# Swin block on one core: TensorE's side jobs regrouped by tile shape, with PSUM banks, element-wise steps and stores placed anew

## Chip, cores and metric

One core of a Trainium2 chip runs the kernel. The metric is the device time of one launch in microseconds, the median of three runs. The kernel before takes 2514.27 us (2513.03 to 2517.35).

## What is computed

The input x is (32, 56, 56, 64) in f32. The reference is one Swin block with shifted 7x7 windows and eight heads of width 8:

```python
y = _ln(x, norm1_w, norm1_b)
y = jnp.roll(y, (-3, -3), axis=(1, 2))
win = y.reshape(B, nWh, 7, nWw, 7, C).transpose(0, 1, 3, 2, 4, 5).reshape(B * nW, N, C)
qkv = (win @ qkv_w.T).reshape(B * nW, N, 3, h, d).transpose(2, 0, 3, 1, 4)
attn = jnp.einsum('bhnd,bhmd->bhnm', q, k) * scale + bias[None]   # + shift mask
attn = jax.nn.softmax(attn, axis=-1)
out = jnp.einsum('bhnm,bhmd->bhnd', attn, v) ... @ proj_w.T + proj_b
x = shortcut + roll(out, (3, 3))
z = _ln(x, norm2_w, norm2_b)
return x + (gelu(z @ fc1_w.T + fc1_b) @ fc2_w.T + fc2_b)
```

## The kernel before, in words

The 2048 windows are cut into NSB = 128 super-blocks of 16 windows. A super-block is worked in U = 8 rounds (k = 0 to 7) of two windows with all heads. Every engine has a program of its own, written by hand as `body(i, m)` for super-block i; the engines meet through semaphores only. VectorE (DVE), ScalarE (ACT), GpSimd (POOL) and SyncE (SP) run four bodies in a hardware loop. TensorE's program is written out in full for all super-blocks.

**The spine.** In round k TensorE does `scores` (tile S, 16 matmuls, in rounds 3 and 7 two more for the mask), `scores_T` of two rounds earlier (tile ST), at most one or two side jobs ("fillers"), `shift` (two matmuls that add the row maximum to ST) and `times_v` of four rounds earlier (tile O). Between them, `neg_max` (VectorE, line 541) takes the row maxima of S, `shift_rows` (GpSimd, 295) makes a diagonal matrix of them, and `exp` (ScalarE, 385) takes the exponential of ST. S has one PSUM bank: `scores` of round k+1 waits for `neg_max` of round k. ST has two.

**The fillers** do the rest of the block for super-blocks at other stages; the letters in `body` name them: a = i+1, f = i+2, n = i+3, c = i-1, d = i-2, e = i-3, g = i-4. `turn_y`, `turn_o`, `turn_z` and `turn_back` are transposes; `project_qk` and `project_v` make q, k and v of the next super-block; `project_out` is the projection behind attention; `fc1` runs in two halves, `fc2` in one. All fillers share the four-bank PSUM tile M.

**Tile shapes.** The part of the array that a matmul uses follows from rows and columns of its weights. The spine's matmuls and `fc2` use all rows and a half of the columns (weights 128x49, 121x49, 113x49, 128x64). The four turns use all rows and all columns (113x128, 128x113). `project_qk`, `project_out` and `fc1` use half of the rows and all columns (64x128, 64x113). `project_v` uses half of both (64x49).

**q and k go through DRAM.** `high_parts` (ScalarE) and `low_parts` (VectorE, 532) split q and k in two f16 parts; `write_parts` (SP) stores them and `read_parts` reads them back, spread over heads, ten transfers a super-block. `scores` of round 0 waits for the first five of them (semaphore `s_q`). SP also issues the loads of x and the stores of the result.

**Other steps.** VectorE: `ln1_*` and `ln2_*` (sums, centering, variance), `evac_yT`, `evac_zT`, `normalise` (twice), `add_attention`, `result`. ScalarE: squares, `place_v`, `evac_oT`, `evac_m`, and `gelu` twice, each change between exp and gelu with a table load. GpSimd: reciprocal roots, row scaling, `keep_residual`.

TensorE's body before, where fillers stand in the rounds:

```python
if k == 0 and on_chip(g): turn_back(g)        # ahead of scores
if k == 0: project_qk(a, d)
if k == 1: project_v(a)
if k == 2: fc1_low(e, a, d)
if k == 3: fc1_high(e, a, g)
if k == 4: turn_y(f, e)      # and fc2(e) behind times_v
if k == 5: turn_o(c, e, a)
if k == 6: project_out(c, f)
if k == 7: turn_z(d, e, a)
```

Of the kernel before, what the change touches and what calls it, by code (L numbers as in the profile page):

```python
# [14 lines left out]
N = WIN * WIN  # L15
SHIFT = 3
HEADS = 8
D = 8
# [3 lines left out]
W0 = 64  # L22
# [18 lines left out]
def swin_block(nc, x, norm1_w, norm1_b, wqk_T, wv_T, proj_wT, proj_b, cpb_w1T, cpb_b1, cpb_w2T, h_times,  # L41
# [4 lines left out]
    with ctx:  # L46
# [162 lines left out]
        def _(sp):  # L209
# [66 lines left out]
        def _(pool):  # L276
# [54 lines left out]
            def body(i, m):  # L331
                f, n, d = i + 2, i + 3, i - 2
                for k in range(U):
                    if k == 0 and on_chip(i):
                        keep_residual(i, m)
                    if on_chip(i):
                        shift_rows(i, k)
                    if k == 1 and on_chip(f):
                        ln1_rows(f)
                    if k == 4 and on_chip(d):  # L340
                        ln2_rstd(d)
                        ln2_rows(d)
                    if k == 7 and on_chip(n):
# [5 lines left out]
        def _(act):  # L349
# [13 lines left out]
            def high_parts(u):  # L363
                act.wait_ge(s_qk, u + 1)
                if later(u):
                    for b in range(2):
                        act.wait_ge(s_parts[b], 32 * u)
                nc.scalar.activation(hl[:, 0].rearrange("m b a t -> m a b t"),  # L368
                                     M[:, 0:2, 0:HT].rearrange("m a (b t) -> m a b t", b=2), ACT.Copy).then_inc(s_hi, 1)

            def place_v(u, r):
                act.wait_ge(s_vp, u + 1)
                dst = vx[r % RING][:].rearrange("n s h f -> n (s h) f")
                for e in range(2):
                    rows = slice(W0 * e, W0 * e + N)
                    nc.scalar.activation(dst[rows, :, D * e:D * e + D].rearrange("n (a s) d -> n a s d", a=2),  # L376
                                         M[rows, 2:4, 0:256].rearrange("n a (s d) -> n a s d", d=D),
# [22 lines left out]
            def gelu(u, c):  # L400
                act.wait_ge(s_f, 2 * u + 1 + c)
                if c == 0 and later(u):
# [4 lines left out]
            def evac_m(u):  # L407
# [3 lines left out]
                nc.scalar.activation(mT[:, :, 0:N], M[:, 2, 0:HT].rearrange("c (w n) -> c w n", n=N),  # L411
                                     ACT.Identity, bias=fc2b[:, 0:1]).then_inc(s_mT, 1)

            def body(i, m):
                a, n, c, d, e = i + 1, i + 3, i - 1, i - 2, i - 3
                for k in range(U):
                    if k == 0 and on_chip(a):
                        high_parts(a)
                    if k == 1 and on_chip(a):
                        place_v(a, m + 1)  # L420
                    u, j = at_unit(i, k, 2)
                    if on_chip(u):
                        exp(u, j)
                    if k == 0 and on_chip(d):
                        square2(d)
                    if k == 2 and on_chip(e):
                        gelu(e, 0)
                        gelu(e, 1)
                    if k == 3 and on_chip(n):
                        square1(n)  # L430
                    if k == 4 and on_chip(c):
                        evac_oT(c)
                    if k == 5 and on_chip(e):
                        evac_m(e)
# [4 lines left out]
        def _(dve):  # L439
# [90 lines left out]
            def low_parts(u):  # L530
                dve.wait_ge(s_hi, u + 1)
                V.tensor_tensor(hl[:, 1].rearrange("m b a t -> m a b t"),
                                M[:, 0:2, 0:HT].rearrange("m a (b t) -> m a b t", b=2),
# [55 lines left out]
            def result(u, r):  # L589
# [3 lines left out]
                V.tensor_tensor(res[r % 2][:], M[0:R, 3, :], xres[r % RING][:].rearrange("r p c -> r (p c)"),  # L593
                                ALU.add).then_inc(s_res, 1)

            def body(i, m):
                a, f, n, c, d, e, g = i + 1, i + 2, i + 3, i - 1, i - 2, i - 3, i - 4
                for k in range(U):
                    if k == 0:
                        if on_chip(d):  # L600
                            ln2_sum(d, m + 2)
                        if on_chip(e):
                            evac_zT(e)
                        if on_chip(c):
                            normalise(c, 0)
                    if k == 4 and on_chip(c):
                        normalise(c, 1)
                    if on_chip(i):
                        neg_max(i, k)
                    if k == 0:  # L610
                        if on_chip(g):
                            result(g, m)
                        if on_chip(d):
                            ln2_center(d, m + 2)
                    if k == 1:
                        if on_chip(a):
                            low_parts(a)
                        if on_chip(d):
                            ln2_var(d)
                    if k == 2 and on_chip(n):  # L620
                        ln1_sum(n, m + 3)
                    if k == 3 and on_chip(n):
# [317 lines left out]
```

## Time and profile before

| | |
|---|---|
| median of three runs | 2514.27 us |
| the profiled execution | 2507.17 us, its span 2505.4 us |
| granted TensorE clock, mean of the span | 0.989 of full speed |
| TensorE busy (PE) | 2260.3 us, 90%, 66954 matmul records (an f32 product that takes two passes counts as two) |
| its weight loads (PEld) | 1741.6 us, 70% |
| GpSimd (POOL) | 1792.0 us, 72% |
| VectorE (DVE) | 1769.7 us, 71% |
| ScalarE (ACT) | 1541.6 us, 62% |
| DMA queue 1 | 138118 packets, 210.58 MB, 41.1% of 16 engines |

Busy time is a union of intervals, and matmuls are pipelined: one matmul's interval covers the starts of those behind it. What a group of matmuls costs TensorE is therefore read from the start of its first matmul to the start of what follows. "issue" names idle time in front of which the profile shows nothing that was waited for.

### The profile page before, as it was taken

The numbers are of one execution on the slowest core, as the hardware profiler recorded it, in microseconds if no ns is written. First come the engines' busy times: TensorE is split into PE (matmuls) and PEld (weight loads), VectorE is DVE, ScalarE is ACT, GpSimd is POOL, SyncE is SP. The second block draws the span as 40 slices with busy tenths as digits, with TensorE's granted clock in tenths as the row PEclk, the third lists the DMA queues.
The fourth block names the chain that finished last, engine by engine and source line by source line (L and its number), as shares of the span: only waits on it lengthen the run. The fifth ranks groups of instructions, "written<-read, shape, count | busy, mean of one in ns | idle before, by whom it ended". The sixth has DMA issues, their size and how long they took to land.

```text
span 2505.4 us, 156242 instructions
## 1 busy us (share of the span) xinstructions
PE 2260.3 (90%) x66954; PEld 1741.6 (70%) x66954; DVE 1769.7 (71%) x3277; ACT 1541.6 (62%) x2433; POOL 1792.0 (72%) x1680
## 2 busy tenths in 40 slices
PE   0528999999999999999999999999999999999998
PEld 0527677777777777777777777776777777777775
DVE  0046777777777777777777777777777877777774
ACT  0005666667666667666766666666667667666665
POOL 0417777777777777777777777777777777777774
PEclk9999999999999999999999999999999999999999
DMA  2014444444444444344444444444444444444441
GB/s 79 0 31 95 87 94 90 94 93 97 93 99 90 98 90 93 86 95 94 101 89 100 87 100 87 94 90 94 89 88 95 95 95 98 91 91 92 90 93 41
DMA packets 138664, 219.38 MB, mean 88 GB/s; under 512 B 30182, under 2 KB 96476, under 8 KB 137948
## 3 DMA queue, kind: packets, MB, share of 16 engines
q1 hardware_dynamic: 138118, 210.58, 41.1%
q8 instruction: 528, 8.65, 1.6%
q14 instruction: 18, 0.15, 0.0%
HBM read 133.40 MB, written 77.07 MB: 84 GB/s over the span
## 4 chain that ended last, share of the span: by engine, by line
PE 83%; issue 5%; ACT 5%; SPq 2%; DVE 2%; POOL 1%; DMA 0%; ACTq 0%; DVEq 0%; POOLq 0%
PE O L706 13%; PE ST L692 11%; PE S L670 9%; PE M L714 8%; PE ST L686 8%; PE M L779 7%; PE M L801 7%; PE M L765 5%; PE M L748 5%; PE M L732 5%; PE M L809 3%; ACT L404 3%; ACT gl L404 2%; SPq L220 2%; PE S L648 2%
## 5 line engine op out<-in xcount | busy, mean ns | idle before, releaser
L295 POOL TENSOR_TENSOR nmd<-diag,nm 121x392 f16<-121x392 f16 x1024 | 898.0, 885 | 443.6 <-DVE nm L541 423.3
L541 DVE TENSOR_REDUCE nm<-S 121x8 f16<-121x392 f32 x1024 | 576.5, 563 | 385.6 <-PE S L674 185.5
L385 ACT ACTIVATE pT<-ST 113x392 f32<-113x392 f32 x1024 | 506.4, 495 | 408.2 <-PE ST L692 403.7
L706 PEld LDWEIGHTS O<-vx,pT 113*49 113x49 f32 x16384 | 552.0, 127 | 62.7 <-issue 21.9
L706 PE MATMUL O<-vx,pT 113*49 113x18 f32 x16384 | 529.8, 197 | 18.7 <-issue 16.2
L686 PE MATMUL ST<-qp,kp 128*49 128x49 f16 x16384 | 396.7, 186 | 30.2 <-issue 28.1
L670 PE MATMUL S<-kp,qp 128*49 128x49 f16 x16384 | 395.9, 186 | 25.6 <-issue 16.1
L670 PEld LDWEIGHTS S<-kp,qp 128*49 128x49 f16 x16384 | 318.8, 104 | 98.5 <-issue 70.2
L692 PE MATMUL ST<-nmd,shiftw 121*49 121x392 f16 x2048 | 362.6, 350 | 1.4 <-POOL nmd L295 0.9
L686 PEld LDWEIGHTS ST<-qp,kp 128*49 128x49 f16 x16384 | 330.3, 103 | 42.8 <-issue 34.2
L692 PEld LDWEIGHTS ST<-nmd,shiftw 121*49 121x49 f16 x2048 | 107.3, 101 | 285.3 <-issue 144.3
L368 ACT ACTIVATE hl<-M 128x784 f16<-128x784 f32 x128 | 105.5, 824 | 278.7 <-PE M L732 278.7
L315 POOL TENSOR_TENSOR xres<-xin,projb 113x512 f32<-113x512 f32 x128 | 204.9, 1601 | 94.5 <-DVE res L593 90.8
L302 POOL TENSOR_TENSOR rstd<-veps,mhalf 113x8 f32<-113x8 f32 x128 | 209.6, 1637 | 83.2 <-DVE veps L521 83.2
L779 PE MATMUL M<-zT,w 64*128 64x392 f32 x1024 | 246.8, 555 | 3.6 <-issue 1.9
L404 ACT ACTIVATE gl<-M,b 128x784 f32<-128x784 f32 x256 | 220.8, 911 | 4.9 <-PE M L779 3.4
L322 POOL TENSOR_TENSOR rstd<-veps,mhalf 113x8 f32<-113x8 f32 x128 | 210.9, 1648 | 12.2 <-DVE veps L580 12.2
L801 PE MATMUL M<-gl,w 128*64 128x392 f32 x1024 | 194.0, 500 | 3.4 <-ACT gl L404 3.4
L376 ACT ACTIVATE vx<-M 49x512 f32<-49x512 f32 x256 | 155.2, 606 | 33.6 <-PE M L748 24.0
L404 ACT ACT_TABLE_LOAD x126 | 161.7, 1283 | 2.3
L385 ACT ACT_TABLE_LOAD x126 | 161.7, 1283 | 2.2
L547 DVE RECIPROCAL rec<-O 113x32 f32<-113x32 f32 x256 | 90.2, 352 | 85.0 <-PE O L706 85.0
(93 smaller groups left out, 3406.0 us busy)
## 6 DMA issues: line engine op xcount, KB each, us to landing
parts<-hl SPq DMA_DIRECT2D x512, 98.0 KB, 2.7
qp<-parts SPq DMA_DIRECT2D x512, 98.0 KB
xin<-in_x SPq DMA_DIRECT2D x256, 98.0 KB
kp<-parts SPq DMA_DIRECT2D x256, 98.0 KB
kp<-parts SPq DMA_DIRECT2D x512, 49.0 KB
out<-res SPq DMA_DIRECT2D x256, 98.0 KB
onehot<-in_c_onehot SPq DMA_DIRECT2D x2, 2082.5 KB
w<-in_fc_wT SPq DMA_DIRECT2D x3, 64.0 KB
```

Of the source, the lines that this page charges most:

```text
L295: nc.gpsimd.tensor_tensor(nmd[j % LAG][:], diag[:], nm[j % LAG][:].unsqueeze(2).broadcast_to([RM, 2 * 4, N]), ALU.mult).then_inc(s_nmd, 1)
L302: nc.gpsimd.tensor_tensor(rstd1[:], veps1[:], mhalf[:], ALU.pow).then_inc(s_rs1, 1)
L322: nc.gpsimd.tensor_tensor(rstd2[:], veps2[:], mhalf[:], ALU.pow).then_inc(s_rs2, 1)
L385: nc.scalar.activation(pT[j % LAG][:].rearrange("k w h q -> k (w h q)"), ST[0:R, j % 2, 0:HK], ACT.Exp).then_inc(s_e, 1)
L404: nc.scalar.activation(gl[:, c], M[:, 2 * c:2 * c + 2, 0:HT], ACT.Gelu, bias=b1[:, c:c + 1]).then_inc(s_g, 1)
L541: V.tensor_reduce(nm[j % LAG][:], S[0:RM, 0:HK].rearrange("q (h n) -> q h n", n=N), AX_X, ALU.max, negate=True).then_inc(s_nm, 1)
L670: mm = MM(S[W0 * e:W0 * e + N, N * (4 * w + hp):N * (4 * w + hp + 1)], q[:, 2 * hp + e, t], key[:, 2 * hp + e, t], start=(w == 0 and hp == ...
L686: MM(ST[W0 * e:W0 * e + N, j % 2, N * (4 * w + hp):N * (4 * w + hp + 1)], key[:, 2 * hp + e, t], q[:, 2 * hp + e, t], start=(w == 0 and hp ...
L692: mm = MM(ST[W0 * e:W0 * e + N, j % 2, 0:HK], shiftw[:, variant(r, j), e, :], nmd[j % LAG][:].rearrange("r h n -> r (h n)"), start=False, ...
L706: mm = MM(O[W0 * w:W0 * w + N, (4 * p + hp) * VC:(4 * p + hp + 1) * VC], pT[j % LAG][:, w, hp, :], vx[r % RING][:, window + w, hp, :], sta ...
L779: mm = MM(M[:, 2 * c + h, 0:HT], w1[rows, 128 * c:128 * c + 128], zT[rows, :], start=True, stop=True)
L801: mm = MM(M[C * h:C * h + C, 2, 0:HT], w2[:, c, :], gl[:, c, h, :], start=(c == 0), stop=(c == 1), tile_position=(0, C * h), skip_group_ch ...
```

## The change

The computation and its instructions are the same, but for their order, the PSUM bank that each filler uses, and the semaphores that guard the banks.

- TensorE: `project_out` moves from round 6 into round 0 behind `project_qk` (both with weights of 64 rows); all four turns stand together in round 5; `turn_z` and `fc1` go one stage later (fc1 in rounds 6 and 7, high half first), and `fc2` moves to round 4, for g. Rounds 1 and 3 have no filler, `project_v` is in round 2.
- Banks of M: q and k in banks 2 and 3 (were 0 and 1), v in 0 and 1 (were 2 and 3), fc2 and `turn_back` in bank 0 (were 2 and 3).
- VectorE: `neg_max` comes first in each round; `low_parts` moves from round 1 to round 2, `add_attention` from round 6 to round 0 of the next body, `evac_zT`, `result` and `ln2_var` into round 5 behind `evac_yT`.
- ScalarE: its fillers stand ahead of `exp` in their round; gelu in round 7 in place of 2.
- GpSimd: `ln2_rstd` in round 0, `ln1_rows` and `ln2_rows` in round 2, `keep_residual` in round 5, `ln1_rstd` in round 6.
- SP: the store of the result is issued behind the transfers of q and k, not ahead of them.

```diff
@@ sync body
             if on_chip(n):
                 load(n, m + 3)
-            if on_chip(g):
-                store(g, m)
             if on_chip(a):
                 write_parts(a, m + 1)
                 read_parts(a, m + 1, 0)
                 read_parts(a, m + 1, 1)
+            if on_chip(g):
+                store(g, m)
@@ scalar body
-                    if k == 0 and on_chip(a):
+                    if k == 1 and on_chip(a):
                         high_parts(a)
-                    if k == 1 and on_chip(a):
+                    if k == 3 and on_chip(a):
                         place_v(a, m + 1)
+                    if k == 4 and on_chip(g):
+                        evac_m(g)
+                    if k == 4 and on_chip(c):
+                        evac_oT(c)
+                    if k == 5 and on_chip(d):
+                        square2(d)
+                    if k == 5 and on_chip(n):
+                        square1(n)
+                    if k == 7 and on_chip(e):
+                        gelu(e, 1)
+                        gelu(e, 0)
                     u, j = at_unit(i, k, 2)
                     if on_chip(u):
                         exp(u, j)
...
@@ vector body, as it stands now
                    if on_chip(i):
                        neg_max(i, k)
                    if k == 0:
                        normalise(c, 0); add_attention(d, m + 2)
                    if k == 1: ln2_sum(d, m + 2)
                    if k == 2: low_parts(a); ln1_sum(n, m + 3)
                    if k == 3: normalise(c, 1)
                    if k == 4: ln1_center(n, m + 3); ln2_center(d, m + 2)
                    if k == 5: evac_yT(f); evac_zT(e); result(g, m); ln2_var(d)
                    if k == 6: ln1_var(n)
@@ tensor: the guards that changed
-            def project_qk(u, d):
+            def project_qk(u, d, g):
                 pe.wait_ge(s_yT, u + 1)
-                if on_chip(d):
-                    pe.wait_ge(s_att, d + 1)
+                if on_chip(g):
+                    pe.wait_ge(s_g, 2 * g + 1)
...
-                    mm = MM(M[:, h, 0:HT], wqk[rows, :], yT[rows, :], start=True, stop=True)
+                    mm = MM(M[:, 2 + h, 0:HT], wqk[rows, :], yT[rows, :], start=True, stop=True)
...
+            def project_out(u, i, g):
                 pe.wait_ge(s_oT, u + 1)
+                if on_chip(g):
+                    pe.wait_ge(s_g, 2 * g + 2)
...
+            def fc2(u, a, d):
+                pe.wait_ge(s_g, 2 * u + 2)
                 if on_chip(a):
+                    pe.wait_ge(s_vx, 2 * a + 2)
@@ tensor body
                     if k == 0 and on_chip(a):
-                        project_qk(a, d)
-                    if k == 1 and on_chip(a):
+                        project_qk(a, d, g)
+                    if k == 0 and on_chip(d):
+                        project_out(d, i, g)
+                    if k == 2 and on_chip(a):
+                        room_for_v(a, d)
                         project_v(a)
...
+                    if k == 4 and on_chip(g):
+                        fc2(g, a, d)
+                    if k == 5:
+                        if on_chip(f):
+                            turn_y(f, a)
+                        if on_chip(c):
+                            turn_o(c, a)
+                        if on_chip(e):
+                            turn_z(e, a)
+                        if on_chip(g):
+                            turn_back(g)
+                    if k == 6 and on_chip(e):
+                        fc1_high(e, c)
+                    if k == 7 and on_chip(e):
+                        fc1_low(e, f, g)
                     if on_chip(u2):
                         shift(u2, r2, j2)
                     if on_chip(u4):
                         times_v(u4, r4, j4)
-                    if k == 4 and on_chip(e):
-                        fc2(e)
```

How TensorE's order changes, first around rounds 0 to 2. A row is a group of matmuls; S, ST and O are the spine's tiles. Before, from round 0 (behind its `turn_back`):

```order
L670 MATMUL S<-kp,qp 49x49 x16
L686 MATMUL ST<-qp,kp 49x49 x16
L732 MATMUL M<-yT,wqk 128x392 x2
L692 MATMUL ST<-nmd,shiftw 49x392 x2
L706 MATMUL O<-vx,pT 49x18 x8
L670 MATMUL S<-kp,qp 49x49 x16
L686 MATMUL ST<-qp,kp 49x49 x16
L748 MATMUL M<-wv,yT 49x32 x32
L692 MATMUL ST<-nmd,shiftw 49x392 x2
L706 MATMUL O<-vx,pT 49x18 x8
L670 MATMUL S<-kp,qp 49x49 x16
L686 MATMUL ST<-qp,kp 49x49 x16
```

And the same place now:

```order
L737 MATMUL M<-yT,wqk 128x392 x2
L770 MATMUL M<-wproj,oT 113x64 x8
L694 MATMUL ST<-nmd,shiftw 49x392 x2
L708 MATMUL O<-vx,pT 49x18 x8
L672 MATMUL S<-kp,qp 49x49 x16
L688 MATMUL ST<-qp,kp 49x49 x16
L694 MATMUL ST<-nmd,shiftw 49x392 x2
L708 MATMUL O<-vx,pT 49x18 x8
L672 MATMUL S<-kp,qp 49x49 x16
L688 MATMUL ST<-qp,kp 49x49 x16
L751 MATMUL M<-wv,yT 49x32 x32
```

The projection stands directly behind q and k, a whole round of the spine without a filler comes in between, and v is one round later. The same engine at the turns of round 5, where the spine stood between any two of them before:

```order
L688 MATMUL ST<-qp,kp 49x49 x16
L716 MATMUL M<-ident,y 128x113 x4
L716 MATMUL M<-ident,on 128x113 x4
L716 MATMUL M<-ident,z 128x113 x4
L814 MATMUL M<-ident,mT 113x128 x4
L694 MATMUL ST<-nmd,shiftw 49x392 x2
L708 MATMUL O<-vx,pT 49x18 x8
```

The four turns now follow one another with nothing between. On VectorE, this is what stands between the maxima of rounds 5, 6 and 7 now:

```order
L528 TENSOR_SCALAR yT<-M,n1w,n1b 128x392
L587 TENSOR_SCALAR zT<-M,n2w,n2b 128x392
L594 TENSOR_TENSOR res<-M,xres 113x512
L577 TENSOR_REDUCE ss<-sq 113x8
L581 TENSOR_SCALAR veps<-ss 113x8
L542 TENSOR_REDUCE nm<-S 121x8
L518 TENSOR_REDUCE ss<-sq 113x8
L522 TENSOR_SCALAR veps<-ss 113x8
L542 TENSOR_REDUCE nm<-S 121x8
```

Behind the turns, five steps are queued ahead of round 6's maximum, where before it was one or two.

## Rows read from the trace of the kernel before

**Rows 1.** Busy time by stretch, 400 to 1000 us: length, busy (matmuls counted), clock, DMA share, GB/s; and the page's row of instruction transfers
```profile
400.00:1000.00 600.00, 578.71 (x17602) 443.33 (x17602) 458.67 (x844) 407.67 (x642) 464.33 (x439) 0.99 0.47 94
...
q8 instruction: 528, 8.65, 1.6%
```

**Rows 2.** Waits of PE: waiter, released by, us in total, times, longest
```profile
PE ST L686 <- issue: 28.1, 37, 2.3
PE O L706 <- issue: 16.2, 22, 2.4
PE S L670 <- issue: 16.1, 30, 1.5
PE M L714 <- ACT gl L404: 12.9, 56, 0.5
```

**Rows 3.** Timeline of PE, round 7: start us, us, line, operation, tiles, count
```profile
1217.38 0.38 PE L686 MATMUL ST<-qp,kp 128*49 128x49 f16 x16
1217.69 0.61 PE L714 MATMUL M<-ident,z 113*128 113x113 f32 x4
1218.22 0.35 PE L692 MATMUL ST<-nmd,shiftw 121*49 121x392 f16 x2
```

**Rows 4.** Timeline of PE, a stretch that ends within a turn (its first two matmuls)
```profile
1231.57 0.37 PE L670 MATMUL S<-kp,qp 128*49 128x49 f16 x16
...
1232.08 0.41 PE L714 MATMUL M<-ident,on 113*128 113x113 f32 x2
```

**Rows 5.** Timeline of PE, rounds 1 and 2 of the next super-block, v to fc1
```profile
1221.91 0.94 PE L748 MATMUL M<-wv,yT 64*49 64x32 f32 x64
1222.77 0.35 PE L692 MATMUL ST<-nmd,shiftw 121*49 121x392 f16 x2
1222.96 0.51 PE L706 MATMUL O<-vx,pT 113*49 113x18 f32 x16
1223.31 0.37 PE L670 MATMUL S<-kp,qp 128*49 128x49 f16 x16
1223.52 0.27 PE L686 MATMUL ST<-qp,kp 128*49 128x49 f16 x8
1224.76 0.29 PE L686 MATMUL ST<-qp,kp 128*49 128x49 f16 x8 [0.97 <-issue]
1224.98 0.93 PE L779 MATMUL M<-zT,w 64*128 64x392 f32 x4
1225.84 0.35 PE L692 MATMUL ST<-nmd,shiftw 121*49 121x392 f16 x2
```

**Rows 6.** Timeline of PE near the start, where a round had no filler
```profile
196.18 0.21 PE L670 MATMUL S<-kp,qp 128*49 128x49 f16 x2 [0.30 <-DVE nm L541]
```

**Rows 7.** Timeline of DVE: that round's maximum, and later the one of Rows 4
```profile
195.57 0.55 DVE L541 TENSOR_REDUCE nm<-S 121x8 f16<-121x392 f32 x1
...
1231.98 0.57 DVE L541 TENSOR_REDUCE nm<-S 121x8 f16<-121x392 f32 x1 [1.50 <-PE S L670]
```

**Rows 8.** Timeline of DVE, from result on in the super-block of Rows 5
```profile
1220.47 0.68 DVE L593 TENSOR_TENSOR res<-M,xres 113x512 f32<-113x512 f32 x1
1221.07 0.68 DVE L571 SCALAR_TENSOR_TENSOR z<-sum,xres 113x512 f32<-113x512 f32 x1
...
1223.26 0.68 DVE L576 TENSOR_REDUCE ss<-sq 113x8 f32<-113x512 f32 x1
1223.97 0.55 DVE L580 TENSOR_SCALAR veps<-ss 113x8 f32<-113x8 f32 x1
1224.43 0.55 DVE L541 TENSOR_REDUCE nm<-S 121x8 f16<-121x392 f32 x1
```

**Rows 9.** Timeline of PE, the projection behind attention
```profile
1215.61 1.01 PE L765 MATMUL M<-wproj,oT 64*113 64x64 f32 x16
```

**Rows 10.** The first trip of q and k through DRAM: low parts on DVE, then PE's wait
```profile
174.77 0.97 DVE L532 TENSOR_TENSOR hl<-M,hl 128x784 f16<-128x784 f32 x1 [1.84 <-ACT hl L368]
...
185.04 0.56 PE L670 MATMUL S<-kp,qp 128*49 128x49 f16 x16 [8.17 <-DMA kp<-parts]
```

More of the change, by code:

```diff
@@ L400, in gelu @@
             def gelu(u, c):
-                act.wait_ge(s_f, 2 * u + 1 + c)
-                if c == 0 and later(u):
+                act.wait_ge(s_f, 2 * u + 2 - c)
+                if c == 1 and later(u):
                     act.wait_ge(s_m, u)
@@ L423, in body @@
                         exp(u, j)
[L424 to L434, printed above, removed]
             rounds(act, body)
@@ L610, in body @@
                     if k == 0:
+                        if on_chip(c):
+                            normalise(c, 0)
+                        if on_chip(d):
+                            add_attention(d, m + 2)
+                    if k == 1 and on_chip(d):
+                        ln2_sum(d, m + 2)
+                    if k == 2:
+                        if on_chip(a):
+                            low_parts(a)
+                        if on_chip(n):
+                            ln1_sum(n, m + 3)
+                    if k == 3 and on_chip(c):
+                        normalise(c, 1)
+                    if k == 4:
+                        if on_chip(n):
+                            ln1_center(n, m + 3)
+                        if on_chip(d):
+                            ln2_center(d, m + 2)
+                    if k == 5:
+                        if on_chip(f):
+                            evac_yT(f)
+                        if on_chip(e):
+                            evac_zT(e)
                         if on_chip(g):
@@ L716, in turn_tokens, with turn_y, room_for_v @@
                 mm.then_inc(sem_out, 1)
[L718 removed]
+            def turn_y(u, a):
                 pe.wait_ge(s_y1, u + 1)
[L720 to L723 removed]
+                if on_chip(a):
+                    pe.wait_ge(s_vx, 2 * a + 2)
                 turn_tokens(1, y1, s_yTp)
[L726 removed]
+            def project_qk(u, d, g):
                 pe.wait_ge(s_yT, u + 1)
+                if on_chip(g):
+                    pe.wait_ge(s_g, 2 * g + 1)
+                else:
+                    if on_chip(d):
+                        pe.wait_ge(s_oT, d + 1)
+                    if later(u):
+                        pe.wait_ge(s_lo, u)
+                for h in range(2):
+                    rows = slice(C * h, C * h + C)
+                    mm = MM(M[:, 2 + h, 0:HT], wqk[rows, :], yT[rows, :], start=True, stop=True)
+                mm.then_inc(s_qk, 1)
+            def room_for_v(u, d):
                 if on_chip(d):
                     pe.wait_ge(s_att, d + 1)
[L730 to L737 removed]
                 elif later(u):
                     pe.wait_ge(s_vx, 2 * u)
[L740 to L741 removed]
             def project_v(u):
@@ L819, in body @@
                     r4 = m if k >= 4 else m + 3
-                    if k == 0 and on_chip(g):
-                        turn_back(g)
                     if on_chip(i):
                         scores(i, m, k)
-                    if k == 1 and on_chip(a):
-                        room_for_v(a, e, g)
                     if on_chip(u2):
```

129 lines of the change are left out of this document (42 added, 87 removed).

## The prediction

> **What bounds the kernel now.** I read the busy shares first. In the 600 us of [rows 1] TensorE is busy for 578.71, VectorE for 458.67, GpSimd for 464.33, ScalarE for 407.67. Then the waits [rows 2]: where TensorE stands still, it mostly waits for nothing that the profile shows ("issue"), and next for gelu. So its own stream sets the end. Its length comes from start to start. [rows 1] count 17602 matmul records in 600 us; a super-block has 523 (66954 of the table above, by 128), so it takes 17.8 us.
>
> **Unit.** Everything below is in us per super-block, and times 127 at the end (128, less what start and tail have out of step).
>
> **Term 1, changes of tile shape: -0.93.** In [rows 3] the turn begins 0.31 behind the start of ST's 16 matmuls. Where the same shape goes on, such a group passes on after 0.21 (S to ST in [rows 5], 1223.31 to 1223.52). Going in costs 0.10. The first step in the turn is long too: two matmuls of a turn are busy 0.41 [rows 4], four 0.61 [rows 3], so the later ones are 0.10 apart, and the first two 0.41 less the 0.27 of one, which is 0.14. Going out: the turn lasts 0.53 from start to start, its four starts spread over 0.14 + 0.10 + 0.10 = 0.34, and what follows comes 0.19 behind the last in place of 0.10. One separate filler thus pays 0.10 + 0.04 + 0.09 = 0.23 for its shape. Before there are nine such visits (turn_back, q and k, v, fc1 twice, y, o, projection, z), now five (q and k with the projection, v, the four turns, fc1 twice); fc2 has the spine's shape in both. Four visits fewer, 4 x 0.23 = 0.93. Bounds: 0.40 if only the way in is saved, 1.1 if each visit is read 0.04 too low. I take 0.93, since the rows show both sides.
>
> **Term 2, the wait for gelu: -0.15.** turn_y waited for gelu to free its bank, 12.9 us in 56 times [rows 2], 0.10; waits too short for the list make it somewhat more (bounds 0 and 0.2). Now y waits for v's evacuation, rounds earlier. Gelu sits in round 7, and q and k of the next round 0 wait for its first half: a tie, which I count as nothing.
>
> **Term 3, S has one bank: +0.35.** A round without filler is 0.21 (S) + 0.21 (ST, as S) + 0.19 (shift) + 0.35 (O) = 0.96, all from [rows 5]. The loop S, maximum, S needs 0.41 from S's start to the maximum's (1231.57 [rows 4] to 1231.98 [rows 7]) and 0.61 from there to the next S (195.57 [rows 7] to 196.18 [rows 6]), together 1.02. Rounds 1 and 3 lose 0.06 to 0.10 each. Round 6 is worse. Behind the last turn VectorE has result 0.60, the variance 0.71 and 0.46, all start to start [rows 8], 1.8 in all; S of round 6 starts about 0.6 after turn_back ends, so its maximum starts some 1.4 later and the next S 0.61 after that, 2.0 to 2.1, where a round with fc1 lasts 0.21 + 0.31 + 0.86 + 0.19 + 0.35 = 1.92 (fc1 0.86 from [rows 5]). That is 0.1 to 0.2 more. Together 0.35, bounds 0.1 and 0.6.
>
> **Term 4, instructions come in pieces: +0.42.** The profile counts 528 instruction transfers for 2 x 66954 matmuls and weight loads [rows 1]: 254 instructions each, nearly all TensorE's. [rows 5] show what such a piece costs. In the 2.2 us up to 1223.7 about 128 matmuls with as many loads went out, then nothing for 0.97: a piece takes some 3.2 us to arrive (estimate from these rows), and a stretch that uses 256 instructions faster than that stops for the difference. The densest stretch before runs from q and k's end to fc1: 36 + 64 + 128 + 36 + 64 = 328 instructions in 2.9 us (a spine group of 16 is 32, v is 128). Now it runs from the projection's end to fc2: 36 + 100 + 64 + 128 + 36 + 104 + 64 = 532 instructions in 5.0 us, since rounds 1 and 3 are bare. A piece of 256 lies wholly within such a stretch (328 - 256) / 256 = 0.28 times a super-block before, and (532 - 256) / 256 = 1.08 times now. The three largest issue rows of [rows 2] are 60.4 us in 89 times, 0.68 a time, 0.47 a super-block, with the small ones near 0.58. I reckon the new sum as 1.08 x 0.68 + 0.25 for pieces that fall elsewhere = 1.0. Bounds: nothing, and 0.8 x 0.97 = 0.78. I take 0.42, nearer to the middle since some dense pieces pass without a stop.
> The Trainium skill says the reverse ("Runtime: NRT & Kernel Launch", Instruction fetch mechanics): crossing a 16 KiB boundary, 256 instructions, is mostly hidden. The trace does not agree, with 60.4 us in three rows. By that rule the term would be zero, the sum -0.74 and the time that of rival A.
>
> **Small terms: -0.01.** The stops of term 4 fall into rounds 1 to 3 and cover part of term 3's waits there, -0.06; the clock, 0.99 in [rows 1], may be granted a little less with more stops, +0.05.
>
> **Costed at nothing.** *q and k through DRAM*: round 0 is 0.21 + 0.31 + 0.86 (q and k, as fc1 in [rows 5]) + about 0.8 (the projection, busy 1.01 with its last matmul's tail [rows 9]) + 0.54 = 2.7, round 1 1.0, and low_parts starts behind round 2's maximum (0.41 + 0.48), 4.6 after round 0's S. The next round 0 comes 16.2 after it if nothing stops (17.8, less 0.6 of issue, 0.2 of clock, 0.93 and 0.15, plus 0.35, in round numbers). The first trip took 10.3 from low_parts to S [rows 10]. So 1.3 is left, and any stop adds to it; with that gone it is rival C. *VectorE in round 0*: it holds the maximum, one normalise and add_attention, and has 2.7. *GpSimd*: eight shift_rows and five steps stay; each result is due two rounds later, at least 1.4 after it is made. *ScalarE*: gelu with its table loads lies between two exps; exp of round 7 ends about when round 1's ST asks for it, where TensorE would wait for the maximum anyway. *Stores*: issued later on SP, behind q and k, with no reader. *Start and tail*: the same chain of steps, 1 us either way.
>
> **Sum.** -0.93 - 0.15 + 0.35 + 0.42 - 0.01 = -0.32, times 127 is -41 us. Against the profiled execution, 2507.2, that is 2466; the median of the runs stands 7.1 above it, so 2473.
>
> **Rivals.**
> *A. Instructions are no hindrance.* Then -0.74, -94 us: 2420. For it: some dense pieces pass freely. Against: the stops of [rows 2]. 0.22.
> *B, slower: the dense stretch starves TensorE.* Each of the 1.08 dense pieces stops for 0.97 as in [rows 5], the total goes to 1.35 with the rest, +0.78; with more stops the clock may stand at its lower level more often, for which I put 0.4 (the 0.99 of [rows 1] is a loss of 0.2). With term 3 at 0.4 it comes to -0.93 - 0.15 + 0.4 + 0.78 + 0.4 = +0.50, +64 us: 2578. It decides from +0.74 on for terms 4 and clock together; just past that point lies 2515 to 2540. For it: two bare rounds around the densest filler. 0.17.
> *C. q and k's trip.* The 10.3 of [rows 10] was on DMA engines with little else to do. If it is 12 under load, each super-block waits about 0.5 at S of round 0, in part in place of term 3: 2520. 0.08.
> *D. The turns cool the clock.* The four turns now take 1.8 us without an ordinary matmul. If the clock fell behind them, rounds 6 and 7 (3.9 us) would run at the lower level, where S's group is busy 0.56 [rows 10] in place of 0.37 [rows 5], half as long again: +2.0, +250 us, 2725. The 0.99 of [rows 1], with four separate turns, speaks against it. 0.03.
> The Trainium skill has the rule behind D ("TensorE: Matmul & The Clock Gate", Part 4: PE-mode transpose): transposes do not count as busy for the clock the way matmuls do. No run so far shows turns side by side.
> *E. The change of shape is not what costs* in term 1, and neighbours save nothing: -0.15 + 0.35 + 0.42, +79 us, 2593. 0.02.
>
> **Numbers.** The forecast has 0.48, its own range 2440 to 2505. With A below and the near part of B and C above, 2405 to 2545 leaves out about 2 in 10. A difference under 0.2%, 5 us, is about what a measurement of this kernel can't tell from none. Faster: 0.48 + 0.22 = 0.70; same 0.07, the edge of B and C; slower 0.23.
>
> **What would show it.** *Term 1*: the four turns take 1.7 to 1.8 us from start to start, and the projection starts right behind q and k (under 0.8 after them). *Term 3*: "DVE nm" as releaser of S in rounds 2, 4 and 7, some tens of us. *Term 4*: issue waits grow from about 75 to about 125 us, mostly in rounds 1 to 4. *Wrong*: issue unchanged (A), issue over 170 us or a clock under 0.97 (B, D), "DMA kp<-parts" in front of S (C), or waits for ScalarE's pT in round 1.

## The result, and the profile after

The changed kernel takes 2558.86 us (median of 4 runs, 2542.95 to 2566.67), beside 2513.65 us for the kernel before in the same comparison. The ratio is 1.019, with an interval of 1.011 to 1.027: it is slower by 1.9%. I had forecast 2473 us with a range of 2405 to 2545, and gave "slower" 0.23. The profiled execution is 2542.95 us, 35.8 above the one before.

The page's first rows and its chain, of the kernel after:

```profile
PE 2187.6 (86%) x66954; PEld 1756.8 (69%) x66954; DVE 1877.4 (74%) x3277; ACT 1515.4 (60%) x2433; POOL 1760.8 (69%) x1680
...
PE 66%; DVE 15%; issue 13%; SPq 2%; POOL 2%; DMA 1%; DVEq 0%; ACT 0%; POOLq 0%; ACTq 0%
```

TensorE is busy 73 us less than before (2260.3) and the span is 36 us longer. So the change of order did shorten TensorE's work, and more than all of it came back as standing still. Of the chain, VectorE has 15% and "issue" 13%.

The waits of PE, kernel after (waiter, released by, us in total, times, longest):

```profile
PE S L672 <- DVE nm L542: 43.1, 126, 1.0
PE ST L688 <- issue: 40.9, 47, 1.7
PE M L751 <- issue: 39.5, 54, 1.2
PE S L672 <- issue: 36.0, 43, 1.6
...
PE O L708 <- issue: 28.9, 30, 1.5
```

Against [rows 2]: the gelu wait of the turn (12.9 us) is gone. A wait for VectorE's maximum, once in nearly every super-block, has come. All issue rows together are 156.2 us, where they were 75.6. The row M L751 is `project_v`.

Timeline of PE, kernel after, one super-block from round 0 to the end of round 6 (start us, us, line, operation, tiles, count):

```profile
1236.37 0.37 PE L672 MATMUL S<-kp,qp 128*49 128x49 f16 x16
...
1236.89 0.93 PE L737 MATMUL M<-yT,wqk 64*128 64x392 f32 x4
1237.65 0.92 PE L770 MATMUL M<-wproj,oT 64*113 64x64 f32 x16
...
1239.03 0.37 PE L672 MATMUL S<-kp,qp 128*49 128x49 f16 x16
...
1240.15 0.39 PE L672 MATMUL S<-kp,qp 128*49 128x49 f16 x16
...
1240.69 0.46 PE L751 MATMUL M<-wv,yT 64*49 64x32 f32 x19
1241.70 0.74 PE L751 MATMUL M<-wv,yT 64*49 64x32 f32 x45 [0.56 <-issue]
...
1244.04 0.36 PE L672 MATMUL S<-kp,qp 128*49 128x49 f16 x13
1245.08 0.23 PE L672 MATMUL S<-kp,qp 128*49 128x49 f16 x3 [0.68 <-issue]
...
1247.74 0.60 PE L716 MATMUL M<-ident,y 113*128 113x113 f32 x4
1248.18 0.55 PE L716 MATMUL M<-ident,on 113*128 113x113 f32 x4
1248.57 0.55 PE L716 MATMUL M<-ident,z 113*128 113x113 f32 x4
1248.96 0.60 PE L814 MATMUL M<-ident,mT 128*113 128x128 f32 x4
1249.49 0.35 PE L694 MATMUL ST<-nmd,shiftw 121*49 121x392 f16 x2
...
1250.03 0.37 PE L672 MATMUL S<-kp,qp 128*49 128x49 f16 x16
...
1252.41 0.40 PE L672 MATMUL S<-kp,qp 128*49 128x49 f16 x16 [0.32 <-DVE nm L542]
```

Read the neighbours first. The projection starts 0.76 after q and k (1236.89 to 1237.65), and the turns step by 0.44, 0.39, 0.39 and 0.53, which is 1.75. Now the bare round 1, from 1239.03 to 1240.15, is 1.12 long. Then two stops: within `project_v`, and within S of round 4. Each stretch between two starts is longer than the idle time in brackets, since the last matmuls' tails count as busy. Last, round 6 runs from 1250.03 to 1252.41, 2.38, and ends on a wait for the maximum.

The means say the same over the run. These are the lengths from S to the next S in us, the mean of 95 super-blocks (20 to 114), worked out from both traces:

```
round      0     1     2     3     4     5     6     7    sum
before   2.01  2.09  2.28  2.14  3.14  1.65  2.12  2.51  17.94
after    2.69  1.16  2.54  1.61  2.81  2.96  2.44  2.06  18.26
```

DVE and POOL of the kernel after, the same place, from VectorE's center steps to round 6's maximum:

```profile
1246.43 1.33 DVE L572 SCALAR_TENSOR_TENSOR z<-sum,xres 113x512 f32<-113x512 f32 x1
...
1249.76 0.68 DVE L594 TENSOR_TENSOR res<-M,xres 113x512 f32<-113x512 f32 x1
1250.36 0.68 DVE L577 TENSOR_REDUCE ss<-sq 113x8 f32<-113x512 f32 x1
1251.07 0.81 DVE L581 TENSOR_SCALAR veps<-ss 113x8 f32<-113x8 f32 x1
1251.80 0.55 DVE L542 TENSOR_REDUCE nm<-S 121x8 f16<-121x392 f32 x1
```

```profile
1245.99 1.22 POOL L295 TENSOR_TENSOR nmd<-diag,nm 121x392 f16<-121x392 f16 x1 [0.95 <-DVE nm L542]
...
1250.59 1.27 POOL L315 TENSOR_TENSOR xres<-xin,projb 113x512 f32<-113x512 f32 x1 [1.43 <-DVE res L594]
```

The maximum starts 1.77 after its S (1250.03). The step `veps` ahead of it takes 0.73 from start to start, where [rows 8] have 0.46, and it ends at 1251.88, together with GpSimd's `keep_residual` (1251.86).

**Where stops fall.** Count TensorE's matmuls, weight loads and semaphore instructions through from the first of the trace, in pieces of 256. Between 400 and 2300 us, 93 steps before and 252 after last over 0.45 us from one start to the next, waits for other engines among them. Of these 73 and 157 stand at one and the same place of a piece, and no other place has more than 3. So the time in which one piece was used can be set against the stop behind it, both from start to start. Pieces used in 2.0 to 2.5 us: 29 before, with a mean stop of 0.89; 88 after, with 1.11. Pieces that took 4 us or more have next to none in either trace (means 0.09 and 0.08). The kernels have 436 and 429 pieces in that time. The transfers can be counted through in the same way: in both traces the instruction at that place never starts less than 2.17 us behind the start of its transfer, in 390 pieces each. This is the picture of term 4, with about a fifth of all pieces dense instead of a fifteenth.

### The profile page after: what moved, and what is told of

Read it like the earlier page. It is cut to its first block, busy times and chain, and to the rows that moved or that the text cites. A ratio compares the mean times of both kernels' runs of the same rounds, so it can differ in the third digit from the quotient of the medians.

```text
span 2541.1 us, 156517 instructions
## 1 busy us (share of the span) xinstructions
PE 2187.6 (86%) x66954; PEld 1756.8 (69%) x66954; DVE 1877.4 (74%) x3277; ACT 1515.4 (60%) x2433; POOL 1760.8 (69%) x1680
## 4 chain that ended last, share of the span: by engine, by line
PE 66%; DVE 15%; issue 13%; SPq 2%; POOL 2%; DMA 1%; DVEq 0%; ACT 0%; POOLq 0%; ACTq 0%
PE O L708 10%; PE S L672 10%; PE ST L688 7%; PE ST L694 7%; PE M L806 6%; PE M L716 5%; PE M L751 5%; PE M L737 4%; PE M L782 4%; PE M L770 4%; DVE ss L577 3%; DVE nm L542 3%; DVE res L594 2%; SPq L220 2%; DVE zT L587 2%
## 5 line engine op out<-in xcount | busy, mean ns | idle before, releaser
L386 ACT ACTIVATE pT<-ST 113x392 f32<-113x392 f32 x1024 | 498.1, 498 | 396.5 <-PE ST L694 393.0
L708 PEld LDWEIGHTS O<-vx,pT 113*49 113x49 f32 x16384 | 561.3, 127 | 97.3 <-issue 57.4
L672 PE MATMUL S<-kp,qp 128*49 128x49 f16 x16384 | 406.6, 187 | 93.6 <-DVE nm L542 43.1
L315 POOL TENSOR_TENSOR xres<-xin,projb 113x512 f32<-113x512 f32 x128 | 162.4, 1269 | 170.2 <-DVE res L594 170.2
L302 POOL TENSOR_TENSOR rstd<-veps,mhalf 113x8 f32<-113x8 f32 x128 | 210.7, 1646 | 97.0 <-DVE veps L522 83.7
L782 PE MATMUL M<-zT,w 64*128 64x392 f32 x1024 | 237.2, 541 | 0.5 <-DVE zT L587 0.3
L412 ACT ACTIVATE mT<-M,fc2b 128x392 f32<-128x392 f32 x128 | 76.4, 597 | 251.6 <-PE M L806 251.6
L806 PE MATMUL M<-gl,w 128*64 128x392 f32 x1024 | 204.3, 513 | 6.9 <-issue 3.9
L393 ACT ACTIVATE oT<-M 128x452 f32<-128x452 f32 x128 | 70.0, 547 | 182.2 <-PE M L716 182.2
L751 PE MATMUL M<-wv,yT 64*49 64x32 f32 x8192 | 136.0, 210 | 39.6 <-issue 39.5
L572 DVE SCALAR_TENSOR_TENSOR z<-sum,xres 113x512 f32<-113x512 f32 x128 | 166.8, 1303 | 0.0
L405 ACT ACT_TABLE_LOAD x126 | 161.7, 1283 | 2.2
```

The source lines that it names most:

```text
L302: nc.gpsimd.tensor_tensor(rstd1[:], veps1[:], mhalf[:], ALU.pow).then_inc(s_rs1, 1)
L386: nc.scalar.activation(pT[j % LAG][:].rearrange("k w h q -> k (w h q)"), ST[0:R, j % 2, 0:HK], ACT.Exp).then_inc(s_e, 1)
L405: nc.scalar.activation(gl[:, c], M[:, 2 * c:2 * c + 2, 0:HT], ACT.Gelu, bias=b1[:, c:c + 1]).then_inc(s_g, 1)
L672: mm = MM(S[W0 * e:W0 * e + N, N * (4 * w + hp):N * (4 * w + hp + 1)], q[:, 2 * hp + e, t], key[:, 2 * hp + e, t], start=(w == 0 and hp == ...
L708: mm = MM(O[W0 * w:W0 * w + N, (4 * p + hp) * VC:(4 * p + hp + 1) * VC], pT[j % LAG][:, w, hp, :], vx[r % RING][:, window + w, hp, :], sta ...
L751: mm = MM(M[W0 * e:W0 * e + N, h, 32 * s:32 * s + 32], yT[rows, N * s:N * s + N], wv[rows, e, :], start=True, stop=True, tile_position=(C ...
```

## Experiments

In each, lines with a minus stood in the kernel named first. All ratios are to the kernel before, on the same chip, with their 95% interval.

**1. The variance of ln2 later.** The changed kernel, with the last two of the five VectorE steps ahead of round 6's maximum (`ln2_var`, its sum and `veps`) moved behind round 7's.

```diff
@@ vector body, k == 5
                             result(g, m)
-                        if on_chip(d):
-                            ln2_var(d)
@@ behind k == 6
+                    if k == 7 and on_chip(d):
+                        ln2_var(d)
```

> The changed kernel with one step of VectorE moved: the variance step ln2_var goes from round 5 (ahead of round 6's maximum) to round 7 (behind its maximum). Theory V (round 6 waits for a maximum that is queued behind result and ln2_var; in the changed kernel's trace the median length of round 6 is 2.47 us where its work needs 1.92): round 6 falls to 1.9 to 2.0, 0.5 us in each of 128 super-blocks, 45 to 65 us faster than the changed kernel, so about 2495 to 2515. Rival I (only the issue stops of TensorE, 156 us in the changed kernel against 76 before, are to blame and would fill any gap that VectorE leaves): less than 15 us faster.

Measured: 1.0057 (1.0027 to 1.0088), 1.3% below the change's 1.0189, some 33 us and less than expected. Round 6 has a mean of 1.95, 0.49 less. Its waits of PE:

```profile
PE ST L688 <- issue: 43.8, 51, 1.7
...
PE M L751 <- issue: 31.7, 56, 2.1
...
PE M L737 <- ACT gl L405: 10.2, 65, 0.4
```

The maximum is gone from the list's head, so VectorE's queue ahead of round 6 is shown to be one of the two causes. Not all of the 0.49 is a gain. Round 0 grew from 2.69 to 2.99, since q and k now reach their bank before gelu has left it. This is the tie that I had counted as nothing.

**2. The projection in the bare round 1.** The changed kernel, with `project_out` (and `add_attention`, which reads it) moved from round 0 to round 1. This splits the dense stretch and gives up one pair of neighbours.

```diff
@@ tensor body
-                    if k == 0 and on_chip(d):
+                    if k == 1 and on_chip(d):
                         project_out(d, i, g)
```

> The changed kernel with project_out moved from round 0 to the bare round 1 (and add_attention of VectorE with it). It costs one more visit of another tile shape, about 0.2 us a super-block (+25 us), and cuts the dense stretch of TensorE's instructions from 532 to 432. Theory I (instruction pieces of 256 that are used up in under 3.5 us stop TensorE for about 1 us each): the pieces that lie wholly in the dense stretch fall from 1.08 to 0.69 a super-block, issue waits fall from 156 to 105 to 120 us, and the time falls by 10 to 35 us net, to about 2525 to 2550. Rival (stops do not follow from the density around v): issue unchanged, time 20 to 30 us longer, 2580 to 2590.

Measured: 1.0306 (1.0231 to 1.0381). Its waits of PE:

```profile
PE S L671 <- DVE nm L542: 56.4, 151, 1.0
...
PE O L707 <- DVE on L552: 26.6, 118, 1.1
PE ST L687 <- issue: 24.7, 33, 1.4
```

Issue falls to 84 us in all from 156, near the 75.6 of the kernel before. That is term 4's cause shown by taking it away: same instructions, one bare round less beside v. Part of the fall can be due to the new waits in these rounds, in which instructions come in as well. And yet the time went up, by 1.2%, which is at the edge of the noise. Rounds 0 and 1 together take 4.52 in the mean for 3.85. Of that, 0.30 is the extra visit (the steps of q and k, ST, shift and the projection, from start to start). Most of the rest is a new wait, with 26.6 us of idle time and more from start to start: round 0 takes 2.30 where its steps add up to 1.91. `times_v` of round 0 writes over what `normalise` reads, and the projection had stood between.

**3. One turn moved in the kernel before.** `turn_y` (and `evac_yT`) from round 4 to round 5, beside `turn_o`.

```diff
@@ tensor body of the kernel before
-                    if k == 4 and on_chip(f):
+                    if k == 5 and on_chip(f):
                         turn_y(f, e)
```

> The kernel BEFORE with one pair of turns side by side: turn_y goes from round 4 to round 5, directly ahead of turn_o (evac_yT of VectorE with it). No round becomes bare, since fc2 stands in round 4. Theory S (a visit of another tile shape costs 0.23 us) plus the wait of turn_y for gelu, 0.15, which goes: 0.38 us a super-block, 40 to 50 us faster than before, so 2465 to 2475. Rival (side by side saves nothing; the gain is eaten by other waits): 0 to 20 us faster.

Measured: 1.0143 (1.0062 to 1.0224). One wait of PE stands out:

```profile
PE O L706 <- DVE on L551: 45.9, 124, 0.6
```

The turn steps by 0.44 beside its neighbour, so the pair saves as forecast, and the gelu wait is gone. But `turn_y` had been what covered `normalise(c, 1)` in round 4, and this wait costs more than its idle time: without the turn the steps of round 4 add up to 2.29 from start to start, and the median is 2.89. That is 0.60 lost, against 0.21 for the pair and 0.16 for gelu.

**4. Two pairs.** The same with `turn_z` behind round 7's `times_v`, right ahead of `turn_back`.

```diff
@@ tensor body
-                    if k == 7 and on_chip(d):
-                        turn_z(d, e, a)
@@ behind times_v and fc2
+                    if k == 7 and on_chip(d):
+                        turn_z(d, e, a)
```

> The previous one with a second pair: turn_z goes from ahead of shift in round 7 to the end of round 7, directly ahead of turn_back. Theory S: a further 0.23 us a super-block, 25 to 30 us, so 2435 to 2448, with issue waits near the 76 us of the kernel before. Rival: no further gain, the same as the previous one within 8 us.

Measured: 1.0112 (1.0075 to 1.0149). The intervals of this and of experiment 3 overlap, so the second pair's worth can't be read from them; the next experiment has it alone.

**5. turn_z beside turn_back alone.** The kernel before with the second edit only, and `evac_zT` behind round 0's maximum.

```diff
@@ vector body, k == 0
-                        if on_chip(e):
-                            evac_zT(e)
@@ behind neg_max, k == 0
+                        if on_chip(e):
+                            evac_zT(e)
```

> The kernel BEFORE with one pair only: turn_z at the end of round 7, directly ahead of turn_back, and VectorE's evac_zT behind round 0's maximum, so that the later turn delays no maximum. turn_y keeps its place in round 4, where it covers the wait of times_v for normalise (26 to 47 us of waits in the two kernels that had taken that cover away). Theory S: 0.23 us a super-block, 25 to 30 us faster than before (ratio 0.988 to 0.990), issue waits unchanged at 70 to 90 us. Rival (a pair saves nothing net): ratio 0.997 to 1.01.

Measured: 0.9974 (0.9935 to 1.0012), which can't be told from no change. Round 7 is 0.26 shorter in the mean (2.25), as a pair should make it, and round 1 is 0.21 longer (2.30): `evac_zT` pushes VectorE's later steps, and round 1's maximum starts 0.87 behind its S in the median, instead of 0.50. Pair and queue cancel.

**6. fc1 as a pair.** The kernel before with both halves of fc1 in round 2 and round 3 bare. The bare round stands apart from v here.

```diff
@@ tensor body of the kernel before
-                    if k == 3 and on_chip(e):
+                    if k == 2 and on_chip(e):
                         fc1_high(e, a, g)
```

> The kernel BEFORE with both halves of fc1 in round 2, so that round 3 is bare, but not beside v: the two halves of fc1 stand between. Theory: -0.23 for the visit, -0.15 for turn_y's wait for gelu, +0.1 for the S loop of the bare round, together -0.28, 30 to 40 us faster than before (ratio 0.984 to 0.988), issue waits stay at 70 to 90 us. Rival (any bare round starves TensorE): issue waits over 110 us, ratio over 1.

Measured: 1.0191 (1.0129 to 1.0253). Its first wait of PE, and the timeline of ACT (an exp of round 2, gelu with its two table loads, the next exp):

```profile
PE M L714 <- ACT gl L404: 118.9, 123, 1.2
```

```profile
1236.06 0.50 ACT L385 ACTIVATE pT<-ST 113x392 f32<-113x392 f32 x1 [2.21 <-PE ST L692]
1236.58 1.28 ACT L404 ACT_TABLE_LOAD   x1
1237.88 1.72 ACT L404 ACTIVATE gl<-M,b 128x784 f32<-128x784 f32 x2
1239.61 1.28 ACT L385 ACT_TABLE_LOAD   x1
1240.90 0.50 ACT L385 ACTIVATE pT<-ST 113x392 f32<-113x392 f32 x1
```

Rounds 2 and 3 together are 4.06 in the mean against 4.42 before. Against that, `turn_y` waits for gelu 0.97 us each time. Issue is 65 us, so a bare round in this place adds no stops. That it is the place which matters, and not the count of bare rounds, isn't shown by this run alone: TensorE also stands still for gelu right behind the bare round, and its next instructions can come in meanwhile.

**7. Both.** Experiments 5 and 6 in one kernel.

> Both of the previous edits together on the kernel BEFORE. Theory: the gains add to 0.5 us a super-block, ratio 0.974 to 0.980 to before, and it beats both kernels. Rival (a wait for VectorE or ScalarE takes the second gain): ratio 0.985 or above.

Measured: 1.0169 (1.0084 to 1.0254), with the gelu wait of experiment 6 (120.0 us).

**8. fc1 as a pair in round 3, round 2 bare beside v.** Meant to feed the dense stretch in the kernel before; gelu moves to round 3 as well.

```diff
@@ tensor body of the kernel before
-                    if k == 2 and on_chip(e):
+                    if k == 3 and on_chip(e):
                         fc1_low(e, a, d)
@@ scalar body: gelu twice, behind square1
-                    if k == 2 and on_chip(e):
+                    if k == 3 and on_chip(e):
```

> As the fc1 pair, but both halves in round 3, so that the bare round 2 stands directly behind v: the dense stretch grows from 328 to 432 instructions with the same matmuls and the same pair. Theory I (density around v): issue waits rise to 110 to 140 us, 35 to 60 us above those of the fc1 pair in round 2; turn_y and round 4 also wait for the later gelu, some 1 to 2 us a super-block, so the time is well above before (ratio 1.03 to 1.10) and only the issue waits are compared. Rival: issue waits the same as in the pair of round 2, within 15 us.

Measured: 1.2061 (1.1994 to 1.2127). The size of it was foreseen by no theory. Its timeline of PE around the wait, and behind it:

```profile
1236.32 0.98 PE L714 MATMUL M<-ident,y 113*128 113x113 f32 x4 [2.74 <-ACT gl L404]
...
1237.56 0.82 PE L706 MATMUL O<-vx,pT 113*49 113x18 f32 x16
```

`turn_y` stands still for 2.74 us, and what follows runs at the lower clock: O's group is busy 0.82 where it is 0.51 elsewhere. Two stretches behind it (length, busy of PE, PEld, DVE, ACT, POOL, clock, DMA share, GB/s):

```profile
1236.30:1241.50 5.20, 5.18 (x59) 3.08 (x61) 0.73 (x2) 2.46 (x3) 1.76 (x2) 0.50 0.47 79
1243.00:1248.00 5.00, 5.00 (x165) 4.45 (x162) 3.79 (x8) 1.93 (x5) 2.76 (x3) 1.00 0.02 3
```

So the gelu chain costs twice, once as a wait (331.7 us in all) and again at 1.2 GHz behind it. Issue is 61 us, but the super-block is now 22 us long, and while TensorE waits for gelu its next instructions come in. This run doesn't settle what it was made for.

**9. Both mends of the change.** Experiments 1 and 2 in one kernel.

> Both single mends of the change together: ln2_var in round 7 and the projection in round 1 (its attention sum with it). Theory 'separate causes' (VectorE's queue ahead of round 6's maximum, and the instruction supply of the stretch with two bare rounds, add up): issue falls to about 85 us as with the projection moved alone, round 6 stays near 1.95 us as with the variance moved alone, and the one new wait of the projection's move stays (times_v of round 0 waits for normalise, about 27 us). Ratio to the kernel before about 1.0057 + 0.0117 = 1.017, less if q and k wait less for gelu. Rival 'one cause' (the stops only shift work against the VectorE queue): issue stays at 120 us or more once round 6 is short again.

Measured: 1.0241 (1.0177 to 1.0304). Issue is 72 us and round 6 1.95, so the two causes are separate. The sum of the single effects, 1.017, lies just below the interval, but has noise of about 0.01 of its own, so the ratios don't show that the two together cost more. The trace has a wait that neither had, while the one for `normalise` is down to 5.8 us:

```profile
PE ST L687 <- ACT pT L386: 57.1, 112, 1.5
```

**10. Experiment 9 with normalise ahead of round 0's maximum.**

```diff
@@ vector body
+                    if k == 0 and on_chip(c):
+                        normalise(c, 0)
                     if on_chip(i):
                         neg_max(i, k)
-                    if k == 0:
-                        if on_chip(c):
-                            normalise(c, 0)
```

> As the one before, with normalise of round 0 ahead of round 0's maximum on VectorE, as the kernel before has it. Theory: round 0 holds q and k (about 1.9 us), so its maximum may come 0.4 us later at no cost, and the wait of times_v for normalise (about 27 us) goes away: 15 to 27 us less than with normalise behind the maximum, ratio 1.005 to 1.01. Rival: the maximum becomes late instead, S of round 1 waits for it, and the time is the same within 0.3%.

Measured: 1.0201 (1.0172 to 1.0229), which can't be told from experiment 9. The wait for normalise is gone (1.3 us) and round 0 is 2.10 instead of 2.33; the wait for exp takes it over (87.7 us). Timeline of ACT, and under it the matmuls that wait:

```profile
1239.49 1.28 ACT L405 ACT_TABLE_LOAD   x1
1240.79 1.72 ACT L405 ACTIVATE gl<-M,b 128x784 f32<-128x784 f32 x2
1242.53 1.28 ACT L386 ACT_TABLE_LOAD   x1
1243.82 0.89 ACT L386 ACTIVATE pT<-ST 113x392 f32<-113x392 f32 x2
```

```profile
1244.37 0.40 PE L686 MATMUL ST<-qp,kp 128*49 128x49 f16 x16 [0.76 <-ACT pT L386]
```

Gelu with its table loads holds ScalarE for 4.3 us (1239.49 to 1243.82). TensorE can be only two rounds ahead of exp, as ST has two banks, and rounds 7 and 0 are now 4.2 together. What the slow rounds 6 and 0 of the changed kernel had hidden is the next bound. The Trainium skill ("ScalarE: Activation LUTs", What ACT_TABLE_LOAD costs) puts a switch at 1283 ns for the load plus a drain of about 1380 ns. The load agrees, 1.28 here; in both timelines what follows a load starts 0.01 to 0.02 us behind it, so no drain shows on this path.

**11. Gelu ahead of exp.** Experiment 6 with gelu twice ahead of round 2's exp on ScalarE.

> The kernel before with both fc1 halves in round 2 and gelu ahead of round 2's exp on ScalarE. Theory 'late start': the wait of turn_y for gelu (119 us with gelu behind exp) is there since gelu starts only behind an exp that itself waits for shift; ahead of it gelu starts at fc1's end, 1 us or more earlier, the wait falls under 40 us and the ratio to 1.000 to 1.006. Rival 'ScalarE's block': gelu twice with two table loads is some 4.5 us, and the exp behind it then comes late for times_v two rounds on: TensorE waits for pT (O) or for ST's bank in rounds 3 to 5, 60 us or more, and the ratio stays above 1.012.

Measured: 1.1208 (1.1179 to 1.1237). The gelu wait is gone and a greater one stands in its place, so the rival "ScalarE's block" holds. It costs more than the wait itself, again with a lower clock (0.934):

```profile
PE ST L686 <- ACT pT L385: 221.1, 125, 2.2
```

**12. The same with turn_z beside turn_back.**

> The same with turn_z beside turn_back as well (which alone gave 0.9974). Theory 'late start': 0.995 to 1.003, the best of the versions with pairs. Rival 'ScalarE's block': above 1.01, with the waits for exp's result named above.

Measured: 1.1208 (1.1190 to 1.1227), with the same wait (237.0 us). No version with pairs is shown to beat the kernel before.

## Why the prediction was wrong

The steps, in us per super-block. "Measured" is read from the profiled executions.

| step | predicted | measured |
|---|---|---|
| term 1, visits | -0.93 | -1.09 (15.50 for 16.59, all steps without stops and waits) |
| term 2, gelu wait of the turn | -0.15 | gone, -0.10 in the list, -0.16 from start to start |
| term 3, round 6 | +0.1 to 0.2 | +0.52 (2.44 for 1.92) |
| term 3, rounds 1 and 3 | +0.06 to 0.10 each | +0.16 (1.12 for 0.96) and +0.09 (1.13 for 1.04, with the mask's two matmuls) |
| term 4, issue | +0.42 | +0.63 as idle time (80.6 us by 127), +0.79 from start to start |
| sum | -0.32 | +0.28 (35.8 us by 127), +0.32 in the mean super-block |

From start to start the measured terms add to -1.09 - 0.16 + 0.52 + 0.25 + 0.79 = +0.31, and the mean super-block grew by 0.32. So terms 3 and 4 failed, and the saving was even larger than forecast. That stops and waits would cover one another (the -0.06) isn't seen.

**Term 1 was right, and it wasn't the step that failed.** The projection comes 0.76 behind q and k ("under 0.8") and the turns take 1.75 ("1.7 to 1.8"). A visit is 0.27 where I had read 0.23, and the four make the 1.1 of the bound. Rival E is out. The fc1 pair of experiment 6 tells the price again: round 2 grew by less than round 3 lost, 0.36 in the mean with a stop or two among it. In the medians rounds 2 and 3 are 2.57 and 1.13 for 1.93 and 2.00, 0.23 less, although the bare round loses some 0.1 to the loop.

**Term 3 failed by its size**, 0.77 where I had 0.35, above my bound of 0.6. Its round 6 rests on 1.8 us of VectorE's steps [rows 8] and on S starting 0.4 behind `result`. In the sample S came 0.27 behind it, and the steps took 0.60 + 0.71 + 0.73 = 2.04. The 0.27 more lies in `veps`, beside a `keep_residual` that this change had moved to the very place. It is held up until `keep_residual` ends (last section), and the row of [rows 8] was a held one too. I costed GpSimd's move at nothing since its results had slack, and didn't ask what it does to VectorE while it runs. Experiment 1 shows that this queue is worth 1.3%. The bare rounds failed by the loop's 0.41 from S to the maximum: it is 0.50 there (1239.03 to 1239.53), and 0.62 from it to the next S. The 0.41 came from round 5. In rounds 0, 1, 3 and 7 of the kernel before, the median was 0.50 to 0.52 already.

**Term 4 was right in mechanism and too small.** The number of dense pieces came: 122 of the 429 were used in under 3 us, 1.17 a super-block for my 1.08. I took 0.68 a stop from [rows 2]. That is a mean of idle time over stops of all kinds, and those of the densest pieces last 1.11 from start to start (88 of them). Rival B had 0.97 for this and +0.78, and from start to start +0.79 came. Experiment 2 takes the stops away and with them 72 us of idle time. Rival B's other leg, the clock, didn't come: 0.988 against 0.989. So the time, 2559 us, lies near the rival's 2578 by a partly different sum, without its 0.4 for the clock and with 0.77 for its 0.4 of term 3. The Trainium skill's "mostly hidden" ("Runtime: NRT & Kernel Launch", Instruction fetch mechanics) doesn't hold here: the stops are 156 us of a 2541 us span, and rival A is out.

**Costed at nothing.** q and k through DRAM: TensorE waits for kp 11.2 us in 3 times, the longest 7.3, where a stall in each super-block was rival C, so C is out. The turns and the clock: D is out, no fall behind 1.75 us of turns. ScalarE: a tie as I said, but hidden only by the losses of term 3. When experiments 1 and 9 mend those, it costs 10.2 us at gelu, then 57.1 at exp. I had let one wait stand as cover for another ("where TensorE would wait for the maximum anyway"), and that cover goes as soon as the first wait is mended.

**Still open.** Why some GpSimd instructions hold `veps` up and its reciprocal roots don't, no run here shows. A kernel that has all of term 1 and none of the uncovered waits was not tried.

## What to carry over

Price each move twice: once for what the job costs in its new place, and once for the latency that it used to cover in the old one, on each engine that had it between a request and its answer. Work out the slack of every other engine against the time hoped for, not the time before. A duration read from a trace holds for the neighbours that it had there: look for the same instruction at its shortest. Where a stream is issued from instructions fetched in pieces, sparse fillers (few long matmuls) do a second job beside dense ones, and a saving that removes them from a dense stretch is partly given back as "issue".

## What the hardware showed that I had not expected

`ln2_center` on VectorE, two inputs from SBUF, has the same shape and work in both kernels. These are its rows by line, first of the kernel after, and for comparison `ln1_center`, which stands just ahead of it:

```profile
L572 DVE SCALAR_TENSOR_TENSOR z<-sum,xres 113x512 f32<-113x512 f32 x128 | 166.8, 1303 | 0.0
...
L513 DVE SCALAR_TENSOR_TENSOR y<-sum,xin 113x512 f32<-113x512 f32 x128 | 88.0, 687 | 2.4 <-issue 2.3
```

Before, it took 0.68 [rows 8]. In the sample it runs from 1246.43 to 1247.76, while `shift_rows` on GpSimd is at work until 1247.21, itself 1.22 long for the 0.84 that it has elsewhere. Each is drawn out while the other runs. The Trainium skill states the rule ("SBUF — State Buffer", SBUF: two separate sides): VectorE with two SBUF inputs and a GpSimd instruction that reads SBUF share a port pair under a lock. The one that starts first has it for its whole length, and the other waits. The trace agrees for z, which ends 0.55 behind `shift_rows` in 123 of 128 super-blocks.

`veps` has one small input, and it is held up as well. These are its rows, in ns the shortest, median and longest, of the kernel after and of experiment 1:

```profile
L581 DVE TENSOR_SCALAR veps<-ss x128: 171/815/821, 233.9 to 2527.2; 113x8 f32<-113x8 f32 x128
L581 DVE TENSOR_SCALAR veps<-ss x128: 170/171/798, 235.2 to 2497.5; 113x8 f32<-113x8 f32 x128
```

By itself it takes 0.17. In the kernel after, `keep_residual` is at work when it starts in 124 of 128 super-blocks, and `veps` ends some 0.03 behind it. In the kernel before, `shift_rows` stood there in 115, and `veps` again ended 0.03 behind it: the 0.55 of [rows 8]. In experiment 1 the reciprocal roots (L302) run beside it in 122, and it takes 0.17. z (79.7 us more than the 87.1 before) and `veps` (32.3 more) are all of the 108 us by which VectorE is busier than before. z's part stood on no path.

The other was the second price of a wait: behind 2.74 us of standing still the granted clock was 0.50 of full speed, 1.2 GHz, over the next 5 us (experiment 8). That span is 512 us longer than before's, and the waits for gelu and the maximum are 370 us of it.
